# Attention times values: the values stationary in four column groups, and the result put in order through HBM

## What is computed

```python
q, k = _rope(q), _rope(k)                      # 16 query heads, 4 key and value heads, 8 wide
scores = jnp.einsum('bhqd,bhkd->bhqk', q, k) / jnp.sqrt(8.0)
valid = (col <= row) & (row - col < 32)        # a window of 32 keys
attn = jax.nn.softmax(jnp.where(valid, scores, -1e9), axis=-1)
out = jnp.einsum('bhqk,bhkd->bhqd', attn, v)
x = x + (out.transpose(0, 2, 1, 3).reshape(Bt, Tt, D) @ Wo + bo)
```

## Time and profile before

| | us |
|---|---|
| median of 3 runs | 510.85 (510.44 to 512.76) |
| the profiled execution, its time | 510.69 |
| its span, first to last instruction | 508.6 |
| PE busy | 438.9 |
| DVE busy | 371.7 |
| ACT busy | 255.1 |
| POOL busy | 224.8 |

### The profile page before, as it was taken

One profiled execution on the slowest core, in us unless ns is written; L12 is line 12 of the kernel. 1 busy time (PEld: TensorE's weight loads), 2 busy tenths in 40 slices (PEclk: granted clock), 3 DMA queues, 4 the chain that ended last, 5 costly groups with the idle time before them and its releaser, 6 DMA issues.

```text
span 508.6 us, 11146 instructions
## 1 busy us (share of the span) xinstructions
PE 438.9 (86%) x3310; PEld 397.3 (78%) x3311; DVE 371.7 (73%) x1010; ACT 255.1 (50%) x536; POOL 224.8 (44%) x252
## 2 busy tenths in 40 slices
PE   2934949789999999999999999899999999997846
PEld 2822448689999999999898989898988788786633
DVE  7858555867877878786868787757878698477682
ACT  2684145445455646555555555346555574653302
POOL 3630043435565556565656464636464363033110
PEclk9965559979999999999999999889999999999789
DMA  8950215424444444444434444424440500002431
GB/s 229 249 196 0 70 62 166 144 89 143 137 141 135 140 128 138 131 134 136 142 130 139 133 142 134 139 93 140 134 100 6 162 1 1 2 0 64 124 103 43
DMA packets 38033, 57.21 MB, mean 112 GB/s; under 512 B 6238, under 2 KB 25442, under 8 KB 37872
## 3 DMA queue, kind: packets, MB, share of 16 engines
q1 hardware_dynamic: 32528, 47.66, 31.3%
q0 software_dynamic: 4608, 8.93, 5.8%
q10 hardware_dynamic: 864, 0.20, 0.2%
HBM read 48.38 MB, written 8.91 MB: 113 GB/s over the span
## 4 chain that ended last, share of the span: by engine, by line
PE 63%; DVE 14%; ACT 11%; issue 8%; another core or an unknown queue 1%; POOL 1%; DVEq 0%; ACTq 0%; POOLq 0%
PE bank L1156 18%; PE bank L1169 11%; PE bank L1120 5%; PE bank L1183 5%; PE bank L1119 4%; PE bank L1194 4%; PE bank L1085 4%; PE bank L1058 3%; PE bank L1098 3%; ACT qbd L913 3%; DVE inter L755 2%; ACT act L938 2%; ACT L937 2%; DVE x_sb L765 1%; ACT S L921 1%
## 5 line engine op out<-in xcount | busy, mean ns | idle before, releaser
L1156 PE MATMUL bank<-xsT,w_sb 128*128 128x128 f32 x1008 | 133.6, 286 | 15.9 <-DVE inter L755 11.1
L1156 PEld LDWEIGHTS bank<-xsT,w_sb 128*128 128x128 f32 x1008 | 122.4, 197 | 21.7 <-issue 18.2
L409 POOL DMA_INDIRECT scratch_ys<-ysb,pair x72 | 77.2, 1073 | 127.0 <-ACT ysb L944 117.8
L402 POOL DMA_INDIRECT xsb<-scratch_xn,token x72 | 74.0, 1027 | 59.4 <-DVE token L587 35.4
L1169 PE MATMUL bank<-w_sb,inter 128*128 x576 | 80.7, 284 | 4.1 <-issue 3.2
L1169 PEld LDWEIGHTS bank<-w_sb,inter 128*128 128x128 f32 x576 | 70.9, 194 | 7.5 <-issue 7.3
L944 ACT ACTIVATE ysb<-bank 128x128 f32<-128x128 f32 x72 | 19.8, 275 | 85.7 <-PE bank L1169 82.6
L1120 PE MATMUL bank<-dv,pO 128*128 128x36 f32 x256 | 50.2, 280 | 1.3 <-ACT h2T_sb L898 1.3
L753 DVE TENSOR_TENSOR inter<-bank,act 64x128 f32<-64x128 f32 x72 | 21.2, 295 | 38.1 <-ACT act L938 32.5
L1120 PEld LDWEIGHTS bank<-dv,pO 128*128 128x128 f32 x256 | 40.4, 198 | 2.8 <-issue 2.8
L1119 PE MATMUL bank<-vbd,pT 128*128 128x36 f32 x224 | 41.8, 271 | 0.0
(11 more groups left out here) (154 smaller groups left out, 811.2 us busy)
## 6 DMA issues: line engine op xcount, KB each, us to landing
w_sb<-in_w SPq DMA_DIRECT2D x72, 448.0 KB
w_sb<-scratch_ys SPq DMA_DIRECT2D x16, 256.0 KB, 3.4
scratch_xn<-xn_sb SPq DMA_DIRECT2D x8, 256.0 KB, 4.9
w_sb<-in_w SPq DMA_DIRECT2D x1, 2048.0 KB, 9.3
out_dram<-x_sb SPq DMA_DIRECT2D x8, 256.0 KB, 2.8
xsb<-scratch_xn,token POOLq DMA_INDIRECT x72
scratch_ys<-ysb,pair POOLq DMA_INDIRECT x72
x_sb<-in_x SPq DMA_DIRECT2D x3, 256.0 KB, 4.1
```

What stands on the lines that cost most here:

```text
L402: nc.gpsimd.indirect_dma_start(xsb[:, j % 3, :], None, xn, bass.IndirectOffsetOnAxis(ap=token[:, j:j + 1], axis=0)).then_inc(slots_in[j % ...
L409: nc.gpsimd.indirect_dma_start(ys, bass.IndirectOffsetOnAxis(ap=pair[:, j:j + 1], axis=0), ysb[:, j % 3, :], None, bounds_check=2 * NTOK - ...
L1156: last = nc.tensor.matmul(to[:, c % EC * P:(c % EC + 1) * P], w13_sb[:, i % 3, c * P:(c + 1) * P], xsT[:, p, :], start=True, stop=True)
```

## The change

The values become the stationary operand (128 x 32, one column group of the array for each of four blocks) and pT and pO the moving one (128 columns). The ones columns go (VW is 32); the row sums come from matmuls of their own, with the mask `vmask_sb` as stationary operand and pT moving, into the second half of `turn_bank`. That makes 16 + 8 = 24 matmuls a batch: quarter 0 has 8 (values of blocks 0 to 3), quarter 1 has 4 (their sums), quarters 2 and 3 the same for blocks 4 to 7. The result lies with (block, value column) on the partitions, so `norm` takes a reciprocal of 128 x 256 and its transpose goes. The order that `project` needs is made through HBM: SP stores `on` into `turned` (128 x 1 KB) and, when that has landed, issues four loads, each of 32 partitions in pieces of 32 elements (128 bytes). In steps 2 to 11 SP does so for batch m - 2 behind the second and third weight load of the step; later the trips stand among the loads of expert results. `project` waits for all four loads. The longest parts of the diff that only name the new tensors and semaphores are left out.

```diff
--- before.py
+++ after.py
@@ -52,7 +52,8 @@
 CHUNK = 16
 CHUNKS = PAIRS // CHUNK
 QKV = (NH + 2 * NKV) * HD
-VW = NKV * HD + NKV
+VW = NKV * HD
+assert VW == WIN
 NO_PAIR = 1e6
 NEG = -1e30
 UP_AT = {(MSTEPS, 0): (0, (0, 1)), (MSTEPS, 1): (0, (2, 3)), (MSTEPS, 2): (1, (0, 1)), (MSTEPS, 4): (1, (2, 3)),
...
@@ -183,7 +184,7 @@
         hotlo = [a.bitcast(BF16).rearrange("p (s j) -> p s j", j=CHUNK)
                  for a in (S.rearrange("p h c -> p (h c)"), spare_hot)]
         past = pO.rearrange("p n g q -> p (n g q)")[:, 0:SLOT_TILES * 7]
-        rsum = sb("rsum", [P, NBLK, NKV])
+        rsum = sb("rsum", [P, T])
         on = sb("on", [P, T])
         outT = sb("outT", [P, T])
         st2 = sb("st2", [P, TPB, 6])
...
@@ -325,9 +326,34 @@
             sp.wait_ge(experts_ready, 1)
             for p in range(3):
                 load_weights(0, p)
-            with sp.Fori(1, SLOT_TILES // 3) as n:
-                for p in range(3):
-                    load_weights(n, p)
+            def store_values(b):
+
+                sp.wait_ge(pv_normed, b + 1)
+                sp.dma_start(turned, on).then_inc(out_stored, 16)
+
+            def load_heads(b):
+
+                sp.wait_ge(out_stored, 16 * (b + 1))
+                for g in range(G):
+                    sp.dma_start(outT[g * 32:(g + 1) * 32, :].rearrange("x (a c q) -> x a c q", a=2, c=4),
+                                 turned.rearrange("(c x) (a g q) -> g x a c q", c=4, a=2, g=G)[g]).then_inc(outT_ready, 16)
+
+            def step(m, tiles=TILES):
+                for i in range(tiles):
+                    load_weights(2 * m + i // 3 + 1, i % 3)
+                    if i == 1 and exists(m - 2):
+                        store_values(m - 2)
+                    if i == 2 and exists(m - 2):
+                        load_heads(m - 2)
+
+            step(0)
+            step(1)
+            step(2)
+            with sp.Fori(3, MSTEPS - 1) as m:
+                step(m)
+            step(MSTEPS - 1, 3)
+            store_values(MSTEPS - 2)
+            load_heads(MSTEPS - 2)
 
             ov = out.rearrange("(t p) d -> p t d", p=P)
@@ -342,10 +368,22 @@
             for i in range(4):
                 load_pairs(i)
+            for b in range(MSTEPS - 1, B - 2):
+                store_values(b)
+                load_heads(b)
+            sp.wait_ge(second_added, 1)
+            load_pairs(4)
+            store_values(B - 2)
+            load_heads(B - 2)
+            for i in range(2, 4):
+                sp.wait_ge(second_added, i)
+                load_pairs(i + 3)
+            store_values(B - 1)
+            load_heads(B - 1)
+            sp.wait_ge(second_added, 4)
+            load_pairs(7)
             for i in range(GROUPS_A):
                 sp.wait_ge(second_added, i + 1)
-                if i + 4 < GROUPS_A:
-                    load_pairs(i + 4)
                 sp.wait_ge(ff_added, i + 1)
                 sp.dma_start(ov[:, 4 * i:4 * i + 4, :], x_sb[:, 4 * i:4 * i + 4, :]).then_inc(stored, 16)
             sp.wait_ge(stored, 16 * GROUPS_A)
...
@@ -588,16 +625,7 @@
             nc.vector.tensor_tensor(pair, found[:, 2], found[:, 0], ALU.add).then_inc(pairs_known, 1)
             dve.wait_ge(gate_in, 64)
-            nc.vector.tensor_copy(identb_sb, ident_sb)
-            nc.vector.tensor_copy(dv[:, :, 0, NKV * HD:VW],
-                                  bc(vmask_sb[:, NKV * HD:VW].rearrange("p (a c) -> p a c", a=1), [P, 2, NKV]))
-            for p in range(2):
-                last = nc.vector.tensor_copy(
-                    vbd[:, p, 1:NBLK + 1, NKV * HD:VW],
-                    bc(vmask_sb[:, NKV * HD:VW].rearrange("p (a c) -> p a c", a=1), [P, NBLK, NKV]))
-            last.then_inc(consts_set, 1)
-
-
+            nc.vector.tensor_copy(identb_sb, ident_sb).then_inc(consts_set, 1)
             def pair_distances():
                 link(nc.vector.scalar_tensor_tensor(tmp[:, 0], sc, -1.0, sc, ALU.mult, ALU.max))
@@ -657,16 +685,15 @@
                 if some(b - 1):
                     dve.wait_ge(pv_psum, b - 1)
                 nc.vector.tensor_tensor(
-                    vbd[:, p, 1:NBLK + 1, 0:NKV * HD], vt.rearrange("p (n c) -> p n c", n=NBLK),
-                    bc(vmask_sb[:, 0:NKV * HD].rearrange("p (a c) -> p a c", a=1), [P, NBLK, NKV * HD]),
+                    vbd[:, p, 1:NBLK + 1, :], vt.rearrange("p (n c) -> p n c", n=NBLK),
+                    bc(vmask_sb.rearrange("p (a c) -> p a c", a=1), [P, NBLK, NKV * HD]),
                     ALU.mult).then_inc(vbd_ready, 1)
             def value_steps(b, p):
                 dve.wait_ge(vbd_ready, b + 1)
                 if some(b - 1):
                     dve.wait_ge(pv_psum, b - 1)
-                nc.vector.tensor_tensor(dv[:, p, :, 0:NKV * HD], vbd[:, p, 1:NBLK + 1, 0:NKV * HD],
-                                        vbd[:, p, 0:NBLK, 0:NKV * HD], ALU.subtract).then_inc(dv_ready, 1)
+                nc.vector.tensor_tensor(dv[:, p], vbd[:, p, 1:NBLK + 1, :], vbd[:, p, 0:NBLK, :], ALU.subtract).then_inc(dv_ready, 1)
             def shift(b, h):
                 row = "p (a k) -> p a k"
@@ -698,15 +725,9 @@
             def norm(b):
                 dve.wait_ge(pv_psum, b + 1)
-                pv = turn_bank[:, 0:NBLK * VW].rearrange("p (n c) -> p n c", c=VW)
-                nc.vector.reciprocal(rsum, pv[:, :, NKV * HD:VW]).then_inc(rsum_ready, 1)
+                nc.vector.reciprocal(rsum, turn_bank[:, T:2 * T]).then_inc(rsum_ready, 1)
                 dve.wait_ge(rsum_ready, b + 1)
-                nc.vector.tensor_tensor(
-                    on.rearrange("p (n h d) -> p n h d", h=NKV, d=HD),
-                    pv[:, :, 0:NKV * HD].rearrange("p n (h d) -> p n h d", d=HD),
-                    bc(rsum.rearrange("p n (h a) -> p n h a", a=1), [P, NBLK, NKV, HD]), ALU.mult).then_inc(pv_normed, 1)
-                dve.wait_ge(pv_normed, b + 1)
-                nc.vector.transpose(outT, on).then_inc(outT_ready, 1)
+                nc.vector.tensor_tensor(on, turn_bank[:, 0:T], rsum, ALU.mult).then_inc(pv_normed, 1)
             def residual(b):
                 dve.wait_ge(wo_psum, b + 1)
@@ -1113,16 +1134,19 @@
                     pe.wait_ge(dv_ready, b + 1)
                     if some(h2T_out):
                         pe.wait_ge(h2T_ready, h2T_out)
-                for n in range(quarter * NBLK // 4, (quarter + 1) * NBLK // 4):
-                    to = turn_bank[:, n * VW:(n + 1) * VW]
-                    if n > 0:
-                        nc.tensor.matmul(to, pT[:, n].rearrange("p g q -> p (g q)"), vbd[:, p, n, :], start=True, stop=False)
-                    last = nc.tensor.matmul(to, pO[:, n].rearrange("p g q -> p (g q)"), dv[:, p, n, :], start=(n == 0), stop=True)
+                a, total = quarter // 2, quarter % 2
+                for i in range(1 if total else 2):
+                    for c in range(4):
+                        n = 4 * a + c
+                        to = turn_bank[32 * c:32 * c + 32, total * T + a * P:total * T + (a + 1) * P]
+                        weights = (pO if i else pT)[:, n].rearrange("p g q -> p (g q)")
+                        values = vmask_sb if total else dv[:, p, n, :] if i else vbd[:, p, n, :]
+                        last = nc.tensor.matmul(to, values, weights, start=(i == 0), stop=(i == 1 or total == 1))
                 if quarter == 3:
                     last.then_inc(pv_psum, 1)
             def project(b, vt_out):
-                pe.wait_ge(outT_ready, b + 1)
+                pe.wait_ge(outT_ready, 16 * G * (b + 1))
                 pe.wait_ge(vt_ready, vt_out)
                 if some(b):
                     pe.wait_ge(x1_ready, b)
@@ -1308,7 +1332,7 @@
     older = (np.arange(WIN)[None, :] > (p % WIN)[:, None]).astype(np.int32)
     newer = (np.arange(WIN)[None, :] >= (p % WIN)[:, None]).astype(f32)
     qmask = np.where((p // HD % NKV)[:, None] == np.arange(NKV), 1.0 / np.sqrt(f32(HD)), 0.0).astype(f32)
-    col = np.concatenate([np.repeat(np.arange(NKV), HD), np.arange(NKV)])
+    col = np.repeat(np.arange(NKV), HD)
     vmask = ((p // WIN)[:, None] == col).astype(f32)
     tri = (p[:, None] < p[None, :]).astype(f32)
     rev = np.broadcast_to(E - np.arange(E), (P, E)).astype(f32)
...
```

More of the change, by code:

```diff
@@ L73, in layer @@
 def layer(nc, x, wqkv, bqkv, wo, bo, g1, b1, g2, b2, wf1, bf1, wf2, bf2, gate, w13, w2,
-          ident, cosf, sinf, older, newer, qmask, vmask, tri, rev, tilegrid, places, column, row, xn, ys, out):
+          ident, cosf, sinf, older, newer, qmask, vmask, tri, rev, tilegrid, places, column, row, xn, ys, turned, out):
     F32, F32R, BF16, I32 = mybir.dt.float32, mybir.dt.float32r, mybir.dt.bfloat16, mybir.dt.int32
@@ L238, in layer @@
             sem("chosen"), sem("rowmax_ready"), sem("shifted"), sem("pO_ready"), sem("dv_ready"))
-        exp_ready, pT_ready, pv_psum, rsum_ready, pv_normed = (sem("exp_ready"), sem("pT_ready"), sem("pv_psum"),
```

(6 more changed lines are left out.)

## The result

The changed kernel takes 502.3 us (median of 4 runs, 501.6 to 503.6), the kernel before 510.6 beside it (508.9 to 512.8): a ratio of 0.984, with an interval of 0.982 to 0.987. It is faster by 1.6%. The forecast of 520 had the wrong sign; the time lies in its range.

A forecast was written before the change was run, and what follows sets the result against it. TensorE's queue was taken to bound the kernel (PE busy 86%). Matmuls -5.3, changes of shape +13.0, DVE +1.0 and HBM tail +0.5 gave +9.2 us on 510.85, forecast 520, range 498 to 553.

The forecast's parts named there:

- The matmuls: `attend`'s 24 matmuls a batch overlap two at a time: 2.69 us against 3.02, so -5.3 us for 16 batches.
- my cheap end: Lower bound for `attend`'s matmuls: four at a time, 1.34 us a batch.
- The changes of shape: On TensorE, each passage between `attend`'s quarters and full-array matmuls costs 0.12 us; 108 of them, +13.0 us.
- Rival (1): In `attend`, four groups really run at once: 485 us if shape changes are free, 498 at 0.12 each; chance 0.12.
- DVE: `norm`'s longer reciprocal, net of the lost transpose, is hidden in the loop and counts in batch 15's tail: +1.0 us.
- The way through HBM: Store and four loads a batch, 8.0 us a trip: hidden in the loop, +0.5 us in the tail.
- the +0.5: Cost in us taken for batch 15's trip through HBM in the tail, between 0 and 3.
- (3): In `attend`, column groups run one after another: 550 us, or 563 with 0.12 for each shape change; chance 0.25.
- (4): Transfers get in the way: 1,024 short pieces a batch, four more hiccups like ACT's wait before copying y; 537 us, chance 0.07.
- the sign against me: The forecast is wrong on the transfers if ACT's waits for stores of y grow; no size given.

## Why the prediction was wrong

**The matmuls: the step that failed.** "... the second has to wait for the group's first to stream, and matmuls start in order in every timeline I read. Only the second half of one can then lie beside the first half of the next." The first clause fits the runs: with one group each recorded matmul takes 0.111. The second did not. I had seen starts in order only on the full array, and made it a rule for groups. The run with the blocks in another order shows that it is none. This term is 16 x (1.34 - 3.02) = -26.9 instead of -5.3, my cheap end, and 21.6 us of the miss. The pitch of 0.056 that I took is what two groups give (0.058); four give half of it.

**The changes of shape** came out as sized: 0.12 forecast; 0.09 to 0.10 going in and 0.11 to 0.13 coming out. Some luck was in it, since 0.12 was a choice between 0 and 0.28 that no row decided. 108 of them at 0.11 are 12 us; the 0.14 from joining them in pairs would make it 15. The Trainium skill (TensorEngine Tiling, Key Properties) has a change of tiling mode drain TensorE; the timelines agree that there is a stop, and give its price, which is not the 0.28 I set for a full drain. Rival (1) named this combination, four at once and stops of 0.12, and gave 498 at a chance of 0.12. The case was in the list, and its chance was too small: nothing spoke against it but that one step, which no row showed for groups.

**DVE.** The reciprocal takes 1.73 to 1.76 us, forecast 1.74 from two shorter ones. In the loop it costs nothing, as said. Outside it costs 5 us, not 1.0, the second term that was wrong: I netted the transpose against it and counted it for batch 15 alone, but its length is not hidden in step 2, in steps 12 and 13 and behind them, and each of these pays 0.8 to 1.4. The slack left in the loop was 0.31 us in most steps; I had 0.2. It held, and with twice the reciprocal it was used up, and 1.16 of the 1.8 us more were paid in each step.

**The way through HBM.** Hidden in the loop, as said. In the tail the trip took 5.9 us, near the fastest landing both ways (5.6), not 8.0; its four issues cost 0.63 each instead of 0.45; nothing that counted waited for it, so 0 in place of the +0.5.

**The sum again, on the chips of the experiments:** -26.9 + 12 + 5 + 0 = -9.9, with -10.8 measured. The first two terms are -14.9, and PE's busy time, which has both, fell by 15.3 on the first chip. With 0.14 a stop the sum would be -6.9, and it leaves out the transpose of 0.45 us a batch that DVE lost, which no run tested alone; so it agrees to within some 3 us, not better. On the first chip the gain is 8.3. PE's waits for `inter` are longer there for both kernels alike (11.1 and 10.1 us, against 4.9 and 5.1). The profiled executions show where the two gains differ. The loop gains 6.6 us there and 5.9 elsewhere, but 4.0 of the 6.6 are the long step of before; three steps of the changed kernel, those with ACT's waits below, take 25.65 to 26.15 us, and four others 24.96 to 25.22, 0.6 to 0.8 below before's 25.8, as the step on the other chips is by 0.75. In step 13 the granted clock fell in the changed kernel there, which costs 1.45 of the 2.5 us between the gains if it happens in each execution there and in few elsewhere. One profile for each kernel can't say whether it does; so how the 2.5 us divide stays open.

**Rivals (3) and (4).** One after another is refuted by the timeline and by the run that forces it: 545 there. On the chips of the experiments the transfers did not get in the way: leaving the whole trip out changes nothing. On the first chip ACT's waits ahead of its copy of y did grow, which I had named as the sign against me: 8.4 us in three waits, before 3.1 in one. The waits of the changed kernel, us in total, times, longest:

```profile
ACT ysb L965 <- remote: 8.4, 3, 2.8
```

The profile doesn't name what ended them; the program has only the last product and the store of an earlier y to wait for there. On the other chips neither kernel has one, with the same short pieces, so these alone don't cause them; whether they do so together with something of the first chip wasn't tried.

## What to carry to other kernels

Four column groups with 32 stationary columns each ran fully beside one another, f32 halves included, in both orders of issue tried; count a quarter of the full-array pitch for each, and 0.1 us for every passage between group work and full-array work (measured with 128 rows and 128 moving columns of f32). So put group work together, up to the point where it stops covering another engine's copy. For an engine that is off the critical path in the loop, work out the slack of the loop and the length of the head and tail separately: the same reciprocal was free in every step of the loop and paid in four places outside it, and in one of them its wait can bring the clock down too.

## What the runs showed of the hardware

Four recorded f32 matmuls with 128 x 32 stationary and 128 moving columns, in four groups, start within 0.02 us of one another when the program goes round the groups and within 0.04 when it goes group by group; the next four start 0.11 to 0.13 us after the first four in both. An f32 matmul is two recorded ones in each group, and with all four groups at work a recorded one takes 0.028 us.

At the granted clock of 0.50 (1.2 GHz) the groups still overlap. The table by windows and the timeline of PE, changed kernel on the first chip:

```profile
463.50:465.50 2.00, 1.85 (x25) 1.50 (x26) 1.96 (x8) 1.29 (x2) 0.00 (x0) 0.50 0.05 12
...
464.05 0.68 PE L1144 MATMUL bank<-pO,dv 128*32 128x128 f32 x8
464.48 0.68 PE L1144 MATMUL bank<-pT,vmask_sb 128*32 128x128 f32 x8
465.09 2.95 PE L1207 MATMUL bank<-h2T_sb,wf_sb 128*128 128x512 f32 x4
```

Eight take 0.43 us (464.05 to 464.48), twice 0.22. The last eight with the way out take 0.61, so 0.18 for the way out, against 0.11 to 0.13 at the full clock.
